# Sixteen output stores of a cross-attention and routed-FFN kernel, issued by GpSimd as indirect DMAs in place of SyncE's strided DMAs

## The chip, the cores and the metric

The kernel runs on one core of one Trainium2 chip. The metric is device time in microseconds (us) of one execution; the time given for a kernel is the median of several runs.

## The reference

What is computed, cut to its core (two batches of 1024 tokens, 256 wide, 64 context keys, 16 heads, 12 experts, the top 3 of them for each of three routers):

```
x = x + attention(layernorm(x), ctx, mask)           # Wq, Wk, Wv, Wo and their biases
xf = layernorm(x)                                    # 2048 rows of 256
C1, C2, C3 = softmax over the top 3 of (xf @ P_w.T) @ U1.T, U2.T, U3.T   # [2048, 12] each
h = gelu(sum_e C1[:, e] * (xf @ W1[e].T))
y = sum_e C2[:, e] * (h @ W2[e].T) + C3 @ b2
return x + y                                         # [2, 1024, 256] float32
```

## The kernel before

The 2048 rows are cut into T = 16 tiles of 128 rows, eight for each batch (TPB = 8). All rows lie in `x_all` [128 partitions, 16 tiles, 256]: tile t holds, on partition p, row 8p + j of batch b, with t = 8b + j. The attention stage adds its result into `x_all`, the expert stage adds the second layer's result into it, and that tile is then stored to the output.

Each engine has a program of its own, written out by hand, and the programs meet only in semaphores. After about 116 us (the attention stage) the expert stage runs, one tile in 17.75 us:

- TensorE (`experts` in the tensor block) multiplies six pairs of experts for layer 1 of tile t + 1 and six pairs for layer 2 of tile t. Each product is six matmuls of 512 columns (`split_product`, L920). Between the pairs stand small steps, among them `transpose_xf(t + 2)` (L1025), which waits for `xf`.
- VectorE (`experts` in the vector block) weighs and sums the products (`sum_pair`, L815), ends a layer with `last_sum` (L820), and between them runs the statistics of tile t + 2 (L595 to L598), `normalise2` (L602, writes `xf`), the router's `find_top` and `combine_weights` (L774 to L793, with `w_at_e` at L787) and `move_weights` (L801).
- GpSimd has three small steps for each tile, in the loop at L429: `inverse_deviation` (L355, L357, writes `rstd`, for which `normalise2` waits), `exponentials` (L406) and `split_c3` (L417, L422).
- SyncE issues all loads but three. Once the last weights are in flight, it has only the stores: `store(b, j, sums)` at L309 waits on `acc`, the count of VectorE's sums, until the tile's last sum is written, and issues one DMA of 128 rows of 1 KB (L311). Two loops run over the tiles, and the last store stands by itself. The program ends when all stores have landed (`stored` at 16 * T).

The semaphore `acc` counts SUMS = 13 per layer and tile. `later(t, n)` says that a tile number is at least n or a loop variable. `is_last(t)` picks other buffers for the last tile.

Of the kernel before, what the change touches and what calls it, by code (L numbers as in the profile page):

```python
# [14 lines left out]
P = 128  # L15
# [6 lines left out]
def xattn_ffn_kernel(nc: bass.Bass, x, mask, ctx_t, wq_t, bq, wk_t, bk, wv_t, bv, wo_t, bo,  # L22
# [56 lines left out]
    with ExitStack() as ctx:  # L79
        def sb(name, shape, dt=F32):  # L80
            return ctx.enter_context(nc.sbuf_tensor(name, shape, dt))

        def sem(name):
            return ctx.enter_context(nc.semaphore(name))
# [20 lines left out]
        head_of = sb("head_of", [P, HPC])  # L105
        head_in = sb("head_in", [P, HPG])
        iota_e = sb("iota_e", [P, EXPERTS])
        minus_half = sb("minus_half", [P, 1])
        eps = sb("eps", [P, 1])
        waited = sb("waited", [P, 1])  # L110
# [117 lines left out]
        bv_in, bo_in = sem("bv_in"), sem("bo_in")  # L228

        consts_set = sem("consts_set")  # L230
        setup_dve = sem("setup_dve")
        kt_done, v_done, g_done = sem("kt_done"), sem("v_done"), sem("g_done")
        ident_b_set, wo_hi, b2_hi = sem("ident_b_set"), sem("wo_hi"), sem("b2_hi")
# [39 lines left out]


        x_dram = x.rearrange("b (p j) d -> b p j d", j=TPB)
        out_dram = out.rearrange("b (p j) d -> p b j d", j=TPB)
        mask_dram = mask.rearrange("b (p j) k -> b p j k", j=TPB)
        rows = lambda w: w.rearrange("(c p) n -> p c n", c=C)
        w_dram = [w.rearrange("(c p) e o -> p c (e o)", c=C) for w in (w1_t, w2_t)]
# [5 lines left out]
        def _(sp):  # L285
# [20 lines left out]
                sp.dma_start(stage[:, n % RING, :, :],  # L306
                             w_dram[layer][:, :, pair * 2 * D:(pair + 1) * 2 * D]).then_inc(w_in[n % RING], 16)

            def store(b, j, sums):  # L309
                sp.wait_ge(acc, sums)  # L310
                sp.dma_start(out_dram[:, b, j, :], x_all[:, j + b * TPB, :]).then_inc(stored, 16)  # L311

            for b in range(BATCH):
                with sp.Fori(0, TPB if b < BATCH - 1 else TPB - 1) as j:
                    store(b, j, 2 * SUMS * j + (2 * SUMS * b * TPB + 3 * SUMS))
            store(BATCH - 1, TPB - 1, 2 * SUMS * T)
            sp.wait_ge(stored, 16 * T)


        @block.gpsimd  # L320
        def _(pool):
# [5 lines left out]
            pool.memset(euler[:, :], EULER).then_inc(consts_set, 1)  # L327
            pool.iota(iota_e[:, :], pattern=[[1, EXPERTS]], base=0, channel_multiplier=0,
                      allow_small_or_imprecise_dtypes=True).then_inc(consts_set, 1)
            pool.wait_ge(consts_set, 7)  # L330

            pool.affine_select(out=ident[:, :], in_=ident[:, :], compare_op=ALU.not_equal, fill=1.0, base=0,
# [70 lines left out]
            def exponentials(t):  # L403

                pool.wait_ge(route, ROUTE_STEPS * t + ROUTE_EXP)
                pool.tensor_tensor(top_e[:, :], euler[:, :], top_d[:, :, :].rearrange("p r k -> p (r k)"),  # L406
                                   ALU.pow).then_inc(e_ready, 1)

            def split_c3(t):

                if is_last(t):
                    pool.wait_ge(route, ROUTE_STEPS * T)
                else:
                    pool.wait_ge(c_moved, t + 1)
                if later(t, 1):
                    pool.wait_ge(c3t_done, t)
                pool.tensor_tensor(c3_hlh[:, 0:3:2, 0:EXPERTS].bitcast(F32R),  # L417
                                   weights2(t)[:, 2:3, :].to_broadcast([P, 2, EXPERTS]),
                                   ones[:, 0:2 * EXPERTS].rearrange("p (k e) -> p k e", k=2),
                                   ALU.mult).then_inc(c3_hi, 1)  # L420
                pool.wait_ge(c3_hi, t + 1)
                pool.tensor_tensor(c3_hlh[:, 1, 0:EXPERTS], weights2(t)[:, 2, :], c3_hlh[:, 0, 0:EXPERTS],  # L422
                                   ALU.subtract).then_inc(c3_lo, 1)

            exponentials(0)
            inverse_deviation(1, stats2_ready, var2_ready, rstd2_ready)
            exponentials(1)
            split_c3(0)
            with pool.Fori(2, T) as t:  # L429
                inverse_deviation(t, stats2_ready, var2_ready, rstd2_ready)  # L430
                exponentials(t)
                split_c3(t - 1)
            split_c3(T - 1)


        @block.scalar
# [774 lines left out]
```

## Time and profile before

| | us |
|---|---|
| median of 3 runs | 414.28 (414.12 to 414.6) |
| span of the profiled execution, first to last instruction | 412.4 |
| TensorE busy | 392.4 (95%) |
| VectorE busy | 342.9 (83%) |
| ScalarE busy | 115.8 (28%) |
| GpSimd busy | 110.9 (27%) |

The span leaves out what lies around the first and last instruction; the median of the runs is 1.88 us above it. Busy time counts neither branches, register and semaphore instructions nor the issue of DMAs. A row of the timeline reads: start in us, duration in us, engine, line, operation, output<-inputs, shape, xcount, and in brackets how long the engine was idle before and what released it. PEld is TensorE's weight load, SPq SyncE's queue.

### The profile page before, as it was taken

The page shows a single profiled execution, that of the slowest core. Times are in us where ns is not written, and L with a number is a line of the kernel's source. Part 1 is how long each engine was busy: PE and PEld are TensorE (multiplying, and loading weights), DVE is VectorE, ACT ScalarE, POOL GpSimd, SP SyncE. Part 2 cuts the span into 40 slices and gives each one's busy share as a digit, 9 for nine tenths or more (in the row PEclk, how much of TensorE's full clock was granted, in tenths as well). Part 3 has the DMA queues.
Part 4 walks back from the last instruction along what each step waited for, and adds up shares of the span by engine and source line. Part 5 has one row for each costly group of instructions (what it writes and reads, how often), then busy time and mean ns, then how long its engine had stood idle before and what let it go on. Part 6 is the DMA issues. An engine that isn't in the chain of part 4 may idle for free.

```text
span 412.4 us, 7824 instructions
## 1 busy us (share of the span) xinstructions
PE 392.4 (95%) x2132; PEld 331.0 (80%) x2132; DVE 342.9 (83%) x1036; ACT 115.8 (28%) x263; POOL 110.9 (27%) x165
## 2 busy tenths in 40 slices
PE   4499999999989999999999999999999999999996
PEld 4388988989868888888888888888888888888884
DVE  3998889889885889789897988989789898888875
ACT  3477888888822111010110101011010100101000
POOL 5462755657520220202112020211202112020200
PEclk9999999999989999999999999999999999999999
DMA  7900123131000000000000000000000000000000
GB/s 225 333 2 2 61 92 98 55 102 51 2 0 3 0 2 13 13 0 13 0 13 13 0 13 0 13 0 13 13 0 13 0 13 13 0 13 0 14 0 26
DMA packets 8612, 12.71 MB, mean 31 GB/s; under 512 B 1076, under 2 KB 5016, under 8 KB 8472
## 3 DMA queue, kind: packets, MB, share of 16 engines
q1 hardware_dynamic: 8040, 12.44, 9.1%
q10 hardware_dynamic: 560, 0.13, 0.1%
q8 instruction: 5, 0.08, 0.1%
q14 instruction: 7, 0.06, 0.0%
HBM read 10.47 MB, written 2.10 MB: 30 GB/s over the span
## 4 chain that ended last, share of the span: by engine, by line
PE 89%; DVE 4%; issue 3%; ACT 2%; DMA 1%; POOL 1%; ACTq 0%; DVEq 0%; POOLq 0%
PE banks L920 68%; PE banks L997 5%; PE banks L987 3%; PE banks L962 3%; PE banks L972 2%; PE banks L975 2%; PE banks L977 2%; PE banks L1035 1%; DMA bk_sb<-in_bk_dram 1%; PE banks L1043 1%; DVE q_hl L625 1%; PE banks L1025 1%; PE banks L1008 1%; PE banks L953 1%; DVE s_max L631 1%
## 5 line engine op out<-in xcount | busy, mean ns | idle before, releaser
L815 DVE SCALAR_TENSOR_TENSOR s_d<-banks,c_cur,s_d 128x256 f32<-128x256 f32 x165 | 72.7, 478 | 27.6 <-PE banks L920 23.1
L920 PE MATMUL banks<-w_h,xf_h 128*128 128x512 f32 x204 | 81.8, 401 | 0.0
L920 PE MATMUL banks<-w_l,xf_h 128*128 128x512 f32 x204 | 80.6, 395 | 0.0
L920 PE MATMUL banks<-w_h,xf_l 128*128 128x512 f32 x204 | 80.2, 393 | 0.0
L406 POOL TENSOR_TENSOR top_e<-euler,top_d 128x9 f32<-128x9 f32 x16 | 28.9, 1807 | 185.1 <-DVE top_d L765 185.1
L920 PE MATMUL banks<-w_h,h_h 128*128 128x512 f32 x180 | 73.5, 408 | 0.0
L920 PE MATMUL banks<-w_l,h_h 128*128 128x512 f32 x180 | 71.1, 395 | 0.0
L920 PE MATMUL banks<-w_h,h_l 128*128 128x512 f32 x180 | 71.1, 395 | 0.0
L815 DVE SCALAR_TENSOR_TENSOR sum<-banks,c_new,sum 128x256 f32<-128x256 f32 x160 | 66.6, 476 | 3.2 <-PE banks L920 3.1
L561 ACT ACTIVATE h_h<-banks 128x256 fp32r<-128x256 f32 x15 | 5.8, 385 | 156.5 <-PE banks L1043 156.5
L920 PEld LDWEIGHTS banks<-w_l,xf_h 128*128 128x128 f32 x204 | 38.6, 189 | 8.5
L920 PEld LDWEIGHTS banks<-w_h,xf_l 128*128 128x128 f32 x204 | 38.8, 190 | 7.8
L920 PEld LDWEIGHTS banks<-w_h,xf_h 128*128 128x128 f32 x204 | 38.8, 190 | 7.7
L920 PEld LDWEIGHTS banks<-w_l,h_h 128*128 128x128 f32 x180 | 33.8, 188 | 8.2
L920 PEld LDWEIGHTS banks<-w_h,h_l 128*128 128x128 f32 x180 | 33.9, 188 | 6.9
L920 PEld LDWEIGHTS banks<-w_h,h_h 128*128 128x128 f32 x180 | 33.9, 188 | 6.8
L366 POOL TENSOR_TENSOR w_l<-stage,w_h 128x1024 f32 (+1 forms) x12 | 28.8, 2397 | 32.6 <-ACT w_h L534 32.6
L997 PE MATMUL banks<-v_ext,prob_t 128*128 (+1 forms) x256 | 30.1, 273 | 0.5 <-ACT prob_t L476 0.5
L997 PEld LDWEIGHTS banks<-v_ext,prob_t 128*128 128x128 f32 x256 | 29.9, 192 | 0.7 <-issue 0.7
L571 ACT ACTIVATE xn_t<-xn 128x256 f32<-128x256 f32 x16 | 6.7, 418 | 77.3 <-DVE xn L820 77.3
L631 DVE TENSOR_REDUCE s_max<-banks 128x16 f32<-128x1024 f32 x16 | 19.6, 1223 | 5.6 <-PE banks L977 5.5
L476 ACT ACTIVATE prob_t<-banks 128x512 f32<-128x512 f32 x32 | 17.4, 594 | 17.7 <-PE banks L987 17.6
(126 smaller groups left out, 618.5 us busy)
## 6 DMA issues: line engine op xcount, KB each, us to landing
stage<-in_w_t_dram SPq DMA_DIRECT2D x12, 512.0 KB, 3.7
out_dram<-x_all SPq DMA_DIRECT2D x16, 128.0 KB, 1.9
x_all<-in_x_dram SPq DMA_DIRECT2D x1, 1024.0 KB, 8.0
x_all<-in_x_dram SPq DMA_DIRECT2D x1, 768.0 KB, 7.9
mask_all<-in_mask_dram SPq DMA_DIRECT2D x2, 256.0 KB, 5.1
x_all<-in_x_dram SPq DMA_DIRECT2D x2, 128.0 KB, 3.5
wk_sb<-in_wk_t_dram SPq DMA_DIRECT2D x1, 256.0 KB, 3.7
wq_sb<-in_wq_t_dram SPq DMA_DIRECT2D x1, 256.0 KB, 4.3
```

The source lines that it names most:

```text
L366: pool.tensor_tensor(w_l[:, n, :, :], stage[:, slot, :, :], w_h[:, n, :, :].bitcast(F32), ALU.subtract).then_inc(w_split, 1)
L406: pool.tensor_tensor(top_e[:, :], euler[:, :], top_d[:, :, :].rearrange("p r k -> p (r k)"), ALU.pow).then_inc(e_ready, 1)
L476: nc.scalar.activation(prob_t[:, j:j + HP // 2, :], ps_pt[:, j:j + HP // 2, :], ACT.Copy).then_inc(pt_copied, 1)
L631: dve.tensor_reduce(s_max[:, :], ps_s, AX_X, ALU.max).then_inc(s_maxed, 1)
L815: dve.scalar_tensor_tensor(out=sums[e % 2][:, :], in0=product, scalar=weights[:, e:e + 1], in1=sums[e % 2][:, :], op0=ALU.mult, op1=ALU.ad ...
L920: ins = pe.matmul(dst, a(c), b(c), start=(i == 0), stop=(i == len(terms) - 1))
L962: ins = pe.matmul(ps_q[:, m, :], wq_sb[:, c, m * P:(m + 1) * P], xn_t[:, c, :], start=(c == 0), stop=(c == C - 1))
L972: pe.matmul(banks[:, c, :].rearrange("p (h k) -> p h k", k=KEYS), ident_b[:, :], mask_bias[:, t, :].unsqueeze(1).to_broadcast([P, HPC, KEY ...
L975: pe.matmul(banks[:, c, group * HPG * KEYS:(group + 1) * HPG * KEYS], q_hl[:, c, group, :], kbd_hh[:, b, c, group, :, :].rearrange("p h k ...
L977: ins = pe.matmul(banks[:, c, :], q_h[:, c, :], kbd_l[:, b, c, :, :].rearrange("p h k -> p (h k)"), start=False, stop=True)
L987: ins = pe.transpose(ps_pt[:, j, :], prob[:, 2 * j:2 * j + 2, :].rearrange("p h k -> p (h k)"), ident[:, :])
L997: ins = pe.matmul(ps_v[:, j * 2 * VW:(j + 1) * 2 * VW], prob_t[:, j, :], v_ext[:, b, j, :], start=True, stop=True)
```

## The change

GpSimd fills a table `row_of` [128, 16] of row numbers once, with an iota at the start: entry (p, t) is 1024b + 8p + j. A store is now an indirect DMA that GpSimd issues: the source is tile t of `x_all`, 128 partitions of 256 floats, and each partition's row goes to the row of the output that `row_of[:, t]` names. The rows, their size and their number are those of before. SyncE's stores and its last wait are gone.

In GpSimd's program the loop over tiles 2 to 15 is written out, and iteration t ends with the store of tile t - 3. Behind it stand the last `split_c3` and the stores of tiles 13, 14 and 15, and the wait for all of them.

```
+        row_of = sb("row_of", [P, T], I32)
...
-        out_dram = out.rearrange("b (p j) d -> p b j d", j=TPB)
+        out_rows = out.rearrange("b n d -> (b n) d")
...
-            def store(b, j, sums):
-                sp.wait_ge(acc, sums)
-                sp.dma_start(out_dram[:, b, j, :], x_all[:, j + b * TPB, :]).then_inc(stored, 16)
-
-            for b in range(BATCH):
-                with sp.Fori(0, TPB if b < BATCH - 1 else TPB - 1) as j:
-                    store(b, j, 2 * SUMS * j + (2 * SUMS * b * TPB + 3 * SUMS))
-            store(BATCH - 1, TPB - 1, 2 * SUMS * T)
-            sp.wait_ge(stored, 16 * T)
...
+            pool.iota(row_of[:, :], pattern=[[SEQ, BATCH], [1, TPB]], base=0,
+                      channel_multiplier=TPB).then_inc(rows_set, 1)
+            pool.wait_ge(rows_set, 1)
             pool.wait_ge(consts_set, 7)
...
+            def store(t):
+
+                pool.wait_ge(acc, 2 * SUMS * t + 3 * SUMS if t < T - 1 else 2 * SUMS * T)
+                pool.indirect_dma_start(out=out_rows, out_offset=bass.IndirectOffsetOnAxis(row_of[:, t:t + 1], 0),
+                                        in_=x_all[:, t, :], in_offset=None).then_inc(stored, 16)
+
             exponentials(0)
             inverse_deviation(1, stats2_ready, var2_ready, rstd2_ready)
             exponentials(1)
             split_c3(0)
-            with pool.Fori(2, T) as t:
+            for t in range(2, T):
                 inverse_deviation(t, stats2_ready, var2_ready, rstd2_ready)
                 exponentials(t)
                 split_c3(t - 1)
+                if t >= 3:
+                    store(t - 3)
             split_c3(T - 1)
+            for t in range(T - 3, T):
+                store(t)
+            pool.wait_ge(stored, 16 * T)
```

Two places of GpSimd's program, each as a row before and now. The first is one iteration for a tile, in the expert stage; the names `stats2_ready`, `route`, `c_moved` and `acc` are semaphores that VectorE raises. Before, in the loop:

```order
90 L355 TENSOR_TENSOR var_eps<-mean_var,eps 128x1 [waits stats2_ready]
91 L357 TENSOR_TENSOR rstd<-var_eps,minus_half 128x1 [waits var2_ready]
92 L405 ISA
93 L406 TENSOR_TENSOR top_e<-euler,top_d 128x9 [waits route]
94 L416 REGISTER_ALU [waits c_moved]
95 L417 TENSOR_TENSOR c_hlh<-c_cur,ones 128x2x12 [waits c3t_done]
96 L422 TENSOR_TENSOR c_hlh<-c_cur,c_hlh 128x12 [waits c3_hi]
97 L429 REGISTER_ALU
98 L429 COMPARE_AND_BRANCH
```

And now, from one `split_c3` to the next iteration's `exponentials` (the line numbers are those of the changed kernel, where L413 and L418 are `split_c3`, L424 the store, L351 and L353 `inverse_deviation`):

```order
97 L413 TENSOR_TENSOR c_hlh<-c_cur,ones 128x2x12 [waits c3t_done,c_moved]
98 L418 TENSOR_TENSOR c_hlh<-c_cur,c_hlh 128x12 [waits c3_hi]
99 L424 DMA out_dram<-x_all,row_of 2048x256 [waits acc]
100 L351 TENSOR_TENSOR var_eps<-mean_var,eps 128x1 [waits stats2_ready]
101 L353 TENSOR_TENSOR rstd<-var_eps,minus_half 128x1 [waits var2_ready]
102 L402 TENSOR_TENSOR top_e<-euler,top_d 128x9 [waits route]
```

The store stands between `split_c3` and the two instructions that make the next `rstd`; the loop's register and branch instructions are gone.

The second place is the end of the program. Before, on SyncE, the last store and the end:

```order
28 L311 DMA out_dram<-x_all 128x256
29 L314 REGISTER_ALU
30 L314 COMPARE_AND_BRANCH
31 L311 DMA out_dram<-x_all 128x256 [waits acc]
32 L79 UNCONDITIONAL_BRANCH [waits stored]
```

Now, on GpSimd:

```order
170 L418 TENSOR_TENSOR c_hlh<-c_cur,c_hlh 128x12 [waits c3_hi]
171 L424 DMA out_dram<-x_all,row_of 2048x256 [waits acc]
172 L413 TENSOR_TENSOR c_hlh<-c_new,ones 128x2x12 [waits c3t_done,route]
173 L418 TENSOR_TENSOR c_hlh<-c_new,c_hlh 128x12 [waits c3_hi]
174 L424 DMA out_dram<-x_all,row_of 2048x256 [waits acc] x3
175 L79 UNCONDITIONAL_BRANCH [waits stored]
```

The last three stores and the wait for all sixteen have moved from SyncE's queue to GpSimd's, and the store of tile 12 stands ahead of the last `split_c3`.

## Rows read from the trace of the kernel before

**Rows 1.** The page: the span, and busy time of each engine.

```profile
span 412.4 us, 7824 instructions
PE 392.4 (95%) x2132; PEld 331.0 (80%) x2132; DVE 342.9 (83%) x1036; ACT 115.8 (28%) x263; POOL 110.9 (27%) x165
```

**Rows 2.** The chain that ended last, 400 to 412.4: start, us, what.

```profile
400.52 8.20 PE banks L920 x36
...
409.66 0.42 DVE x_all L820
```

**Rows 3.** TensorE's waits, 116 to 412.4: us in total, times, longest.

```profile
PE banks L920 <- DVE a_l L655: 1.6, 1, 1.6
PE banks L1035 <- DVE x_all L662: 0.6, 1, 0.6
PE banks L997 <- ACT prob_t L476: 0.5, 1, 0.5
```

**Rows 4.** The tile view of the output: stores, ns min/median/max; time to landing.

```profile
L311 SPq DMA_DIRECT2D out_dram<-x_all x16: 338/339/384, 153.8 to 410.1; - x16
...
DMA to landing us min/median/max: 1.9/1.9/2.3
```

**Rows 5.** Timeline of the end: the last store.

```profile
410.11 0.36 SPq L311 DMA_DIRECT2D out_dram<-x_all  x1
```

**Rows 6.** DMA activity, 400 to 412.4 in 40 slices of 0.31 us.

```profile
DMA  0000000006600000000010000000000000057000
```

**Rows 7.** Timeline, GpSimd, one tile of the expert stage.

```profile
313.81 0.23 POOL L417 TENSOR_TENSOR c_hlh<-c_cur,ones 128x24 fp32r<-128x24 f32 x1 [1.09 <-DVE c_cur L801]
314.12 0.21 POOL L422 TENSOR_TENSOR c_hlh<-c_cur,c_hlh 128x12 f32<-128x12 f32 x1
315.96 0.19 POOL L355 TENSOR_TENSOR var_eps<-mean_var,eps 128x1 f32<-128x1 f32 x1 [1.63 <-DVE mean_var L598]
316.23 0.55 POOL L357 TENSOR_TENSOR rstd<-var_eps,minus_half 128x1 f32<-128x1 f32 x1
```

**Rows 8.** Timeline, VectorE, the same tile.

```profile
313.00 0.43 DVE L820 TENSOR_TENSOR x_all<-s_d 128x256 f32 x1
...
313.46 0.18 DVE L801 COPY c_cur<-c_new 128x36 f32<-128x36 f32 x1
...
314.39 0.27 DVE L787 TENSOR_TENSOR w_at_e<-at_e,top_w 128x108 f32<-128x108 f32 x1
...
318.71 0.40 DVE L602 TENSOR_SCALAR xf<-x_all,mean_var,rstd 128x256 f32 x1
```

**Rows 9.** Timeline, TensorE's weight loads, the same tile.

```profile
320.39 0.26 PEld L1025 LDWEIGHTS banks<-ident,xf 128*128 128x128 f32 x2
```

**Rows 10.** Timeline, 111 to 114.5: a GpSimd and a VectorE operation side by side.

```profile
111.36 2.39 POOL L366 TENSOR_TENSOR w_l<-stage,w_h 128x1024 fp32r<-128x1024 f32 x1 [2.23 <-ACT w_h L534]
...
112.03 2.00 DVE L746 TENSOR_TENSOR xf_l<-xf_t,xf_h 128x256 fp32r<-128x256 f32 x1
```

**Rows 11.** Timeline, VectorE: the same operation with GpSimd idle.

```profile
323.29 0.41 DVE L746 TENSOR_TENSOR xf_l<-xf_t,xf_h 128x256 fp32r<-128x256 f32 x1
```

**Rows 12.** Timeline, the start: GpSimd's constants, and who needs them first.

```profile
1.33 0.14 POOL L328 IOTA iota_e<- 128x12 f32 x1
1.62 0.29 POOL L332 TENSOR_SCALAR_AFFINE_SELECT ident<-ident 128x128 f32<-128x128 f32 x1 [0.15 <-POOL iota_e L328]
...
3.59 0.31 ACT L497 ACTIVATE ident_b<-ident 128x128 bf16<-128x128 f32 x1
```

**Rows 13.** Timeline, GpSimd's last two operations.

```profile
387.58 0.24 POOL L417 TENSOR_TENSOR c_hlh<-c_new,ones 128x24 fp32r<-128x24 f32 x1 [2.24 <-PE banks L1050]
387.90 0.21 POOL L422 TENSOR_TENSOR c_hlh<-c_new,c_hlh 128x12 f32<-128x12 f32 x1
```

**Rows 14.** Timeline, TensorE's weight load for `transpose_c3` of the last tile.

```profile
395.82 0.12 PEld L1050 LDWEIGHTS banks<-ident,c_hlh 128*96 128x96 f32 x1
```

**Rows 15.** Timeline, VectorE: the last sum of tile 14.

```profile
401.35 0.42 DVE L820 TENSOR_TENSOR x_all<-s_d 128x256 f32<-128x256 f32 x1
```

More of the change, by code:

```diff
@@ L230, in xattn_ffn_kernel @@
         consts_set = sem("consts_set")
+        rows_set = sem("rows_set")
         setup_dve = sem("setup_dve")
```

## Prediction

> **What bounds the kernel now.** I read the busy times first: TensorE is at work for 392.4 of 412.4 us, and GpSimd, the engine that takes on the stores, for 110.9 [rows 1]. The waits say more than these shares. From 116 us on TensorE waits for another engine three times, 2.7 us in all, each at the passage between the stages [rows 3], so through the sixteen tiles of the expert stage the matmuls stand back to back. The chain that ended last is matmuls up to 408.72, then VectorE's sums, the last of which ends at 410.08 [rows 2]. Behind it only the last store is left: issued at 410.11, and the span ends at 412.4 [rows 1, 5]. A change to the stores can therefore cost time at two places alone: in this tail, where every part of the last store counts in full, and inside the stage, where it counts only once a delay reaches TensorE. The fifteen earlier stores of SyncE delay nobody, so taking them away gains nothing.
>
> **How far the engines can slip.** I follow one tile. GpSimd ends `split_c3` at 314.33 and has nothing until the statistics release it at 315.96: 1.63 us idle. It then makes `rstd` by 316.78, and VectorE takes that at 318.71, 1.93 us later [rows 7, 8]. VectorE ends `xf` at 319.11, and TensorE loads it at 320.39, 1.28 us later [rows 8, 9]. A store placed behind `split_c3` that holds GpSimd for X us is thus free for VectorE up to 1.63 + 1.93 = 3.56 us, and for TensorE up to 3.56 + 1.28 = 4.84 us. Each us above would be paid by TensorE in each of the twelve iterations in which another `rstd` follows a store.
>
> **The change, part by part.**
>
> *The row table at the start.* One iota more, and a wait for it. The iota of before takes 0.14 us, and the operation behind its wait starts 0.15 us after it ends; twice that at most, 0.3 us, moves `ident` from 1.91 to about 2.2 [rows 12]. The first to read `ident` is ScalarE at 3.59, so 1.4 us of slack cover it: 0. Without this cover it would be 0.3 us.
>
> *The loop written out.* It takes register and branch instructions out of a queue that waits 1.63 us in this place anyway [rows 7]: 0.
>
> *Thirteen stores inside the iterations.* The store of tile t - 3 waits on `acc`, but its tile was summed a whole iteration before `split_c3(t - 1)` is released (a tile's last sum stands just ahead of the `c_cur` copy that releases `split_c3`, at 313.00 and 313.46 in the tile shown [rows 8]; the store then takes the tile summed 17.75 us before that one), so the wait is already met and the store costs only X. Queued behind it is `inverse_deviation`, and behind that VectorE and TensorE. What is X? No row of before shows GpSimd issuing a DMA. From below: SyncE holds its queue 0.34 us for the same 128 rows [rows 4]. From above: GpSimd's longest kind of operation, on 1024 elements in each partition, takes 2.39 us in the row shown [rows 10]. The middle is 1.37, and I take 1.4, since writing out 128 row addresses by a program is neither a tiny operation nor a full pass over a large tile. Even the upper end is below 3.56, so `rstd` comes in time: 0.
>
> *Order at the end.* The store of tile 12 stands ahead of the last `split_c3`, at about 385.3. With X = 1.4 it ends near 386.7, before that `split_c3` starts at 387.58; and its result is first loaded at 395.82, 7.7 us after 388.11 [rows 13, 14]. Tile 13 goes out behind it; tile 14 is summed at 401.77 [rows 15], so its store is issued and landed well before 410. All 0.
>
> *The last store.* Before: 0.03 us from the sum to the issue, 0.36 us of issue, and the data on the DMA engines in the two slices from about 410.9 to 411.5 [rows 2, 5, 6]; the semaphore is up 1.9 us (2.3 at most) after the start of the issue [rows 4]. After: GpSimd is woken by VectorE; where it was idle and waited for `c_cur` it needed 0.17 us, from 313.64 to 313.81 [rows 7, 8], about 0.13 more than SyncE. It then needs X to describe the transfer, in place of 0.36. From then on the same 128 rows of 1 KB move and are confirmed, which I take as unchanged. The tail grows by 0.13 + (1.4 - 0.36) = 1.17 us, and by 0.1 to 2.2 us at the two ends of X. I put 0.15 on top for a path that is longer in ways the rows can't show (descriptors that are written to memory and fetched): 1.3 us.
>
> How far the issue itself differs has a price in the Trainium skill (DMA: Bandwidth & Descriptors, "Latency and other measured facts"): about 1 us to the first byte for a DMA from GpSimd against about 0.6 us from SyncE. By that the tail would grow by some 0.4 us and the time would be 414.7; no row of before can confirm it, and the figure is not said to be for 128 separate row numbers.
>
> *Sum.* Profiled execution: 412.4 + 1.3 = 413.7 us of span. With the 1.88 us by which the median of the runs lies above the span: **415.6 us**, 0.3% more.
>
> **The rivals.**
>
> *B. The issue holds VectorE (slower, much).* Rows show that a GpSimd operation can stop a VectorE operation with two inputs in SBUF: `xf_l` started at 112.03 beside a GpSimd operation that ended at 113.75, and took 2.00 us, ending 0.28 us after it, where it takes 0.41 otherwise [rows 10, 11]. The store now starts at about 314.35, and VectorE's next such operation, `w_at_e`, starts at 314.39 and ends at 314.66 [rows 8]. If the issue holds the path for all of X, `w_at_e` ends 0.11 us (108 elements, by the 0.28 for 256) after 314.35 + X, so everything behind it on VectorE is late by X - 0.2. VectorE has next to no idle time up to `xf`, so the 1.28 us of slack there is what counts. With X = 1.4 the delay is 1.2 and just fits. It decides from X = 1.48 on: each of the twelve or thirteen tiles then pays the excess. X = 1.7 gives 0.22 x 13 = 2.9 us plus a tail of 1.6: 418.8. X = 2.39 gives 0.91 x 13 = 11.8 plus 2.3: 428. Against it: the store reads only one number in each partition, and may be a moment behind `w_at_e`.
>
> The page "SBUF — State Buffer" of the Trainium skill ("Who interferes with whom") states this rule: a VectorE instruction with two SBUF inputs and a GpSimd instruction that reads SBUF exclude each other, one of them waiting until the other ends, but GpSimd instructions that only write don't count. The trace agrees with the first half (2.00 against 0.41 us); whether writing descriptors counts as reading, no run here shows.
>
> *C. GpSimd's own lateness (slower).* If X is over 4.84 us, TensorE pays 12 (X - 4.84): at 5.5 us these are 7.9 us, and with a tail of 5.4 us the time is 427.6. Nothing of before lasts so long on GpSimd (2.39 at most). A milder form is a first store that is slow once, on code that GpSimd has not run before: at two and a half times the longest row, 6 us, it costs 1.2 us once and gives 416.8 with the tail of the forecast.
>
> *D. No change that can be measured.* A measurement of this kernel can tell about 0.2%, 0.83 us, from no change. If describing the transfer takes under about 0.9 us, or is overlapped with the moving of the first rows, the tail grows by less than that: X = 0.34 gives 414.5, X = 0.8 gives 415.0. It decides below X = 0.91. For it speaks that fewer than all 128 rows need be described before the first can move; the 1.9 us of before are mostly way and confirmation, not issue [rows 4, 6].
>
> *E. Faster.* Only if the end of the program, with SyncE done early, closes sooner. Nothing in the rows points to it.
>
> *The change may not do what it says*, if the rows are cut into smaller packets. The row table gives 128 distinct rows of 1 KB for each store, as before, so I give this no chance of its own; more packets than before would show it.
>
> **How the numbers follow.** The forecast (tail alone, 415.1 to 416.8, by X from 0.91 to 2.39 and 0.2 for the landing) has 0.56. D has 0.24, B 0.12, C 0.05 and E 0.03. Slower by over 0.2% is forecast, B and C: 0.73. Within 0.2% is D: 0.24. Faster 0.03. For the range I leave out E and the fastest of D at the lower end and stop at 414.6; at the upper end I take in the forecast, C's mild form and B up to X = 1.7, and stop at 418.8. What is left out is about 0.17.
>
> **What would show it.** (1) In the stage TensorE still waits for nobody, and the final matmul ends within 0.3 us of 408.7; if B or C holds, it is later and the wait of L1025 on `xf` appears. (2) `w_at_e` keeps its 0.27 us; B would make it 1 us or more. (3) GpSimd's store has a duration near 1.4 us, and a landing near 3 us from its start, where SyncE's had 1.9. (4) The span ends 3.5 us after the last sum, in place of 2.3. (5) GpSimd's `rstd` is made at the same distance from the statistics. I am wrong if the last sum moves by more than 0.5 us, or if the tail grows by less than 0.8 or more than 2.5 us.

## The result and the profile after

| | before | after |
|---|---|---|
| median, runs on the same chip (us) | 414.44 (4 runs) | 417.17 (4 runs, 416.57 to 417.37) |
| span of the profiled execution (us) | 412.4 | 415.6 |
| from the end of the last sum to the end of the span (us) | 2.32 | 4.76 |

The change makes the kernel slower: the ratio is 1.0063, with a 95% interval of 1.0047 to 1.008. That is 2.7 us, where 1.3 was forecast. (One sentence is needed for all that follows: the executions of most kernels here fall into a main group and one that takes 1.2 to 1.7 us longer, in whose profiles TensorE's granted clock is low at 26 to 32 us; where a few tenths matter I compare main group with main group, and parts of one profile with parts of another.)

The page of after, with the answers to [rows 1]. Columns: busy time, share, instructions; for the queues packets, MB and share.

```profile
span 415.6 us, 7683 instructions
PE 395.4 (95%) x2132; PEld 333.3 (80%) x2132; DVE 341.7 (82%) x1036; ACT 115.6 (28%) x263; POOL 128.8 (31%) x182
...
q1 hardware_dynamic: 5736, 10.34, 7.8%
q0 software_dynamic: 768, 2.10, 1.4%
```

GpSimd is busy for 17.9 us more: the sixteen stores. They move 2.10 MB in 768 packets, 48 for each store. SyncE's queue q1 has 2304 packets fewer than before (8040 there), which were 144 for each store; the rows were not cut smaller.

TensorE's waits from 116 us on, as [rows 3]: the same three, of the same length.

```profile
PE banks L927 <- DVE a_l L662: 1.6, 1, 1.6
PE banks L1042 <- DVE x_all L669: 0.6, 1, 0.6
PE banks L1004 <- ACT prob_t L483: 0.5, 1, 0.5
```

One tile of the expert stage on GpSimd, as [rows 7], now with the store between `split_c3` and `rstd`:

```profile
314.43 0.23 POOL L413 TENSOR_TENSOR c_hlh<-c_cur,ones 128x24 fp32r<-128x24 f32 x1 [1.00 <-DVE c_cur L808]
314.74 0.21 POOL L418 TENSOR_TENSOR c_hlh<-c_cur,c_hlh 128x12 f32<-128x12 f32 x1
315.12 1.15 POOL L424 DMA_INDIRECT out_dram<-x_all,row_of  x1 [0.17 <-issue]
316.64 0.18 POOL L351 TENSOR_TENSOR var_eps<-mean_var,eps 128x1 f32<-128x1 f32 x1 [0.38 <-DVE mean_var L605]
```

The store holds GpSimd from 315.12 to 316.27, and GpSimd is then idle for 0.38 us again, waiting for the statistics. The 1.63 us of [rows 7] had room for it, and `rstd` is not late at all.

The tile view of the output, as [rows 4]: the time that GpSimd is held, in ns (min, median, max), and the time from the start of the issue to the landing.

```profile
L424 POOL DMA_INDIRECT out_dram<-x_all,row_of x16: 960/1150/1299, 173.0 to 411.1; - x16
...
DMA to landing us min/median/max: 2.6/2.8/3.0
```

The end of the chain that ended last, as [rows 2]:

```profile
410.42 0.44 DVE x_all L827
410.85 0.27 issue
411.12 0.96 POOL out_dram L424
```

And the instructions that close each queue, those of line L79, on GpSimd after the change (duration in ns, start in us):

```profile
L79 POOLq COMPARE_BRANCH  x1: 41/41/41, 413.8 to 413.8; - x1
L79 POOLq DRAIN  x1: 1382/1382/1382, 413.9 to 413.9; - x1
```

The same view of before, where SyncE was the last:

```profile
L79 SPq COMPARE_BRANCH  x1: 38/38/38, 412.0 to 412.0; - x1
L79 SPq DRAIN  x1: 7/7/7, 412.2 to 412.2; - x1
L79 POOLq DRAIN  x1: 326/326/326, 387.9 to 387.9; - x1
```

**Where the 3.2 us of span went.** The tail grew by 2.44 us, in three pieces. From the last sum to the issue: 0.28 us in place of 0.03, so +0.25. From the start of the issue until the engine is released by the landing: 411.12 to 413.8, 2.7 us, in place of 410.11 to 412.0, 1.9 us, so +0.8. From there to the end of the span: 1.8 us in place of 0.4, so +1.4. The last is nearly all one instruction. Each queue ends with a DRAIN; SyncE's takes 0.007 us, GpSimd's 1.38 us, and since GpSimd is now the engine that waits for the last landing, its DRAIN lies behind everything. (The 326 ns of GpSimd's DRAIN in the kernel before begin at 387.9, while its last operation runs until 388.11 [rows 13].)

The remaining 0.76 us is the later end of the last sum, 410.84 for 410.08. Little of it came from the expert stage: from the first `top_e` to the last sum it takes 292.5 us before (from 117.56) and 292.7 after (from 118.14). The other 0.58 us were there at 118 us already. Part of that may be the execution that was profiled: TensorE's granted clock at 17 to 20 us was 0.62 in it, and 1.00 in that of before.

### The profile page after: what moved, and what is told of

Same layout as the page of the kernel before. It is cut to its first block, busy times and chain, and to the rows that moved or that the text cites. A ratio compares the mean times of both kernels' runs of the same rounds, so it can differ in the third digit from the quotient of the medians.

```text
span 415.6 us, 7683 instructions
## 1 busy us (share of the span) xinstructions
PE 395.4 (95%) x2132; PEld 333.3 (80%) x2132; DVE 341.7 (82%) x1036; ACT 115.6 (28%) x263; POOL 128.8 (31%) x182
## 4 chain that ended last, share of the span: by engine, by line
PE 89%; DVE 4%; ACT 2%; issue 2%; POOL 1%; DMA 1%; ACTq 0%; DVEq 0%; POOLq 0%
PE banks L927 67%; PE banks L1004 5%; PE banks L969 3%; PE banks L994 3%; PE banks L979 2%; PE banks L982 2%; PE banks L984 2%; PE banks L1042 1%; DMA bk_sb<-in_bk_dram 1%; PE banks L1050 1%; DVE q_hl L632 1%; PE banks L1032 1%; PE banks L1015 1%; PE banks L960 1%; DVE s_max L638 1%
## 5 line engine op out<-in xcount | busy, mean ns | idle before, releaser
L402 POOL TENSOR_TENSOR top_e<-euler,top_d 128x9 f32<-128x9 f32 x16 | 28.9, 1808 | 185.5 <-DVE top_d L772 185.5
L424 POOL DMA_INDIRECT out_dram<-x_all,row_of x16 | 18.0, 1127 | 22.4 <-DVE x_all L827 19.8
```

The costliest lines, as they stand in the source:

```text
L424: pool.indirect_dma_start(out=out_rows, out_offset=bass.IndirectOffsetOnAxis(row_of[:, t:t + 1], 0), in_=x_all[:, t, :], in_offset=None).t ...
```

## The experiments

Theory A (that of the prediction): the cost is the issue of a DMA by GpSimd, 128 row addresses written out by a program, plus a little of landing. Theory B, formed on the profile after: about half of it is the DRAIN of GpSimd, which is work that depends on what GpSimd has issued. (These letters are not those of the prediction's rivals, nor those in the expectation of e4.) The start is a third, small question. All kernels compute the full output. Each ratio is against runs of the kernel before made beside it.

| run | what stores | median us (range, runs) | ratio, 95% | tail us | GpSimd's DRAIN us |
|---|---|---|---|---|---|
| before | SyncE | 414.13 to 414.22, in three rounds | | 2.32 | 0.33, hidden |
| e1 | 15 GpSimd, last SyncE | 415.33 (414.34 to 416.26, 10) | 1.0019, 1.0 to 1.0037 | 2.47 | 1.301, hidden |
| e2 | 16 GpSimd, plain | 416.6 (416.32 to 417.78, 10) | 1.0053, 1.0036 to 1.007 | 4.35 | 1.375 |
| e3 | 15 SyncE, last GpSimd | 416.12 (415.87 to 417.5, 10) | 1.0048, 1.0028 to 1.0067 | 3.79 | 0.149 |
| e4 | 16 GpSimd, SyncE waits | 417.4 (415.86 to 417.72, 10) | 1.0064, 1.0043 to 1.0084 | 3.89 | beside the landing |
| e5 | 16 GpSimd, earlier in the tile | 418.37 (416.91 to 418.46, 4) | 1.009, 1.007 to 1.0111 | 4.78 | 1.382 |
| e6 | 13 stores in 4 pieces | 424.55 (424.31 to 424.83, 4) | 1.0242, 1.022 to 1.0265 | 7.9 | 4.567 |
| e7 | 13 stores in 8 pieces | 513.0 (512.03 to 514.54, 4) | 1.2366, 1.2338 to 1.2394 | 12.1 | 8.814 |
| e8 | SyncE, row table kept | 415.93 (414.23 to 416.4, 12) | 1.0023, 1.0007 to 1.0038 | 2.43 | 0.324, hidden |
| e9 | e1, GpSimd waits too | 416.18 (415.92 to 417.41, 4) | 1.0057, 1.0037 to 1.0077 | 3.8 | 1.301 |
| e10 | the changed kernel again | 417.02 (416.79 to 418.62, 6) | 1.0063, 1.0044 to 1.0082 | 4.69 | 1.382 |
| e11 | half each | 417.34 (416.44 to 418.23, 4) | 1.007, 1.0048 to 1.0091 | 4.03 | 0.729 |
| e12 | 16 GpSimd, drained before the last | 416.45 (415.57 to 417.28, 4) | 1.0062, 1.0042 to 1.0082 | 3.47 | 0.129 |

The tail is the time from the end of the last sum to the end of the span in the profiled execution. It is the sharper measure: the medians also carry the start.

### Only the last store goes back to SyncE

```
+            sp.wait_ge(acc, 2 * SUMS * T)
+            sp.dma_start(out_dram[:, BATCH - 1, TPB - 1, :], x_all[:, T - 1, :]).then_inc(stored_sp, 16)
+            sp.wait_ge(stored_sp, 16)
...
-            for t in range(T - 3, T):
+            for t in range(T - 3, T - 1):
                 store(t)
-            pool.wait_ge(stored, 16 * T)
+            pool.wait_ge(stored, 16 * (T - 1))
```

> The changed kernel, with the store of the last tile given back to SyncE as a strided DMA; GpSimd waits for its own fifteen stores only. Theory (the tail): the whole cost is behind the last sum, namely 0.25 us of waking, 0.8 us of longer landing and a drain of GpSimd's queue of 1.38 us after the last landing. Then this kernel has SyncE's tail again, 2.3 us from the last sum to the end, GpSimd's drain ends long before, and the time is that of the kernel before, within 0.3 us. Rival (the stage): the thirteen stores inside the iterations cost part of it, through GpSimd, VectorE or the DMA engines; then 0.3 to 1 us over the kernel before stay. Second rival (a fixed cost of having software DMAs at all): 1.4 us or more stay.

The tail is 2.47 us (411.83 to 414.3), that of before within 0.15, although fifteen stores are still indirect ones of GpSimd. Its DRAIN, in the view of the instructions of L79, has not gone; it only has cover:

```profile
L79 POOLq DRAIN  x1: 1301/1301/1301, 406.6 to 406.6; - x1
```

So the fifteen stores inside the stage are free, and the tail's cost belongs to the last store and to what GpSimd does behind it. e1 is the nearest to before; in the main group of its executions it is about 0.4 us over it, which is the question of e8.

### All sixteen by GpSimd, but as plain strided DMAs

```
-                pool.indirect_dma_start(out=out_rows, out_offset=bass.IndirectOffsetOnAxis(row_of[:, t:t + 1], 0),
-                                        in_=x_all[:, t, :], in_offset=None).then_inc(stored, 16)
+                pool.dma_start(out_dram[:, t // TPB, t % TPB, :], x_all[:, t, :]).then_inc(stored, 16)
```

> The changed kernel with the sixteen stores still issued by GpSimd, but as plain strided DMAs, without row numbers (the row table is still filled). Theory: the cost belongs to the software path of GpSimd, not to the row numbers. Tail again about 4.8 us, the same drain of about 1.4 us, and the time within 0.4 us of the changed kernel; the issue may be shorter than 1.15 us (0.8 to 1.1). Rival: the row numbers are what costs (reading them, one description per row); then the issue falls to 0.4 us or less and the time falls by 1 us or more.

The tile view of the output:

```profile
L424 POOL DMA_DIRECT2D out_dram<-x_all x16: 542/628/789, 172.3 to 410.5; - x16
...
DMA to landing us min/median/max: 2.2/2.3/2.5
```

The issue takes little more than half as long, 0.63 us, less than the 0.8 to 1.1 that I had expected, and the tail is 4.35 us in place of 4.76. The row numbers thus cost 0.4 us; the other 2.0 us over the tail of before are there without them, a DRAIN of 1.375 us among them.

### Only the last store by GpSimd, as an indirect one

```
 # against the kernel before; the row table is filled as in the change
-                sp.dma_start(out_dram[:, b, j, :], x_all[:, j + b * TPB, :]).then_inc(stored, 16)
+                sp.dma_start(out_dram[:, b, j, :], x_all[:, j + b * TPB, :]).then_inc(stored_sp, 16)
...
-            store(BATCH - 1, TPB - 1, 2 * SUMS * T)
-            sp.wait_ge(stored, 16 * T)
+            sp.wait_ge(stored_sp, 16 * (T - 1))
...
+            store(T - 1)
+            pool.wait_ge(stored, 16)
```

> The kernel before, with only the last tile's store given to GpSimd as an indirect DMA; the other fifteen stay with SyncE, and GpSimd's loop is a loop again. Theory (the tail): all of the cost is back, 2.4 us over the kernel before by the tail's parts. The issue is a first one here, so it may take 1.3 us in place of 0.96. Rival (the stage): less than 2 us. Rival (the drain works off all sixteen stores): the drain is much shorter than 1.38 us, and the time 1 to 1.5 us over the kernel before.

The instructions of L79 on GpSimd:

```profile
L79 POOLq DRAIN  x1: 149/149/149, 413.9 to 413.9; - x1
```

By theory A the whole cost should be here, because the last store is, and I had expected 2.4 us over before. It isn't: the tail is 3.79 us, 1.47 over before and 0.97 less than after, although this one issue took 1.235 us, 0.27 more than the last one of after (0.96). The DRAIN takes 0.149 us in place of 1.382, 1.23 less; with the 0.27 more of issue this makes the 0.97. So the DRAIN's length comes from the DMAs that GpSimd issued before.

### SyncE waits for the sixteen landings

```
             # SyncE
+            sp.wait_ge(stored, 16 * T)
             # GpSimd
-            pool.wait_ge(stored, 16 * T)
```

> The changed kernel, but SyncE waits for the sixteen landings in place of GpSimd; GpSimd goes into its drain right after the last issue. Theory A (the drain is GpSimd's own work after an issue): it runs beside the landing and is over before it, so the span ends about 0.4 us after the landing, and 1.3 us of the 2.4 are gone. Theory B (the drain waits for the DMA's completion and then takes 1.38 us): nothing is gained, within 0.2 us.

The closing instructions of GpSimd and of SyncE:

```profile
L79 POOLq DRAIN  x1: 3579/3579/3579, 410.3 to 410.3; - x1
L79 SPq DRAIN  x1: 7/7/7, 413.3 to 413.3; - x1
```

GpSimd now enters its DRAIN without waiting for the landing; its 3.58 us even begin ahead of the store's own row (410.5), so they hold the issue too. The tail is 3.89 us: 0.87 of the 1.38 us are won, and GpSimd still ends 0.5 us after SyncE. If all of the DRAIN's work could lie beside the landing, the tail would be 3.4. The issue ends at 411.45; 1.38 us of work from there would be over at 412.8, and the DRAIN ends at 413.9, 0.8 us behind the landing. So neither reading of the expectation came out: more was gained than nothing and less than 1.3 us. How much of the work has to come behind the landing, this run doesn't tell.

### Is it the number of DMAs, or how recent they are?

e9 is e1, with GpSimd made to wait for SyncE's last store as well, so that GpSimd's last DMA was issued 10 us before the DRAIN begins, in place of 3.

```
             # on top of e1
             pool.wait_ge(stored, 16 * (T - 1))
+            pool.wait_ge(stored_sp, 16)
```

> As with the last store given back to SyncE, but GpSimd too waits for that store's landing before it goes to the end, so its drain starts when the last software DMA is 7 us old. Theory (the drain is work that depends on how many DMAs GpSimd has issued since the start: 1.38 us after sixteen, 1.30 after fifteen, 0.15 after one): the drain takes 1.3 us again and lies on the path; the tail from the last sum to the end is 2.3 + 1.3 = 3.6 to 3.8 us. Rival (the drain is slow only behind a DMA that has just landed): it takes under 0.3 us and the tail is 2.4 to 2.6 us.

The instructions of L79 on GpSimd, e9:

```profile
L79 POOLq DRAIN  x1: 1301/1301/1301, 412.9 to 412.9; - x1
```

It takes the same 1301 ns as at 406.6, and the tail goes from 2.47 to 3.8: the 1.3 us have lost their cover. The last store, its issue and its landing are those of before. Age doesn't matter, and one more wait in a program cost 1.3 us.

e11 halves the number: even tiles by SyncE, odd ones (with the last) by GpSimd.

```
+            for t in range(0, T, 2):
+                sp.wait_ge(acc, 2 * SUMS * t + 3 * SUMS)
+                sp.dma_start(out_dram[:, t // TPB, t % TPB, :], x_all[:, t, :]).then_inc(stored_sp, 16)
...
-                if t >= 3:
+                if t >= 3 and (t - 3) % 2:
...
-            for t in range(T - 3, T):
+            for t in (T - 3, T - 1):
...
```

> Stores in turn: the eight even tiles by SyncE as strided DMAs, the eight odd tiles, the last among them, by GpSimd as indirect DMAs. Theory (about 0.085 us of drain for each DMA that GpSimd has issued, from 0.15 at one to 1.38 at sixteen): a drain of 0.15 + 7 x 0.082 = 0.72 us, a tail of 4.1 us, 0.65 us less than with sixteen. Rival (a step: any DMA beyond the first brings the full price): 1.38 us and a tail of 4.7.

The same view of e11:

```profile
L79 POOLq DRAIN  x1: 729/729/729, 415.1 to 415.1; - x1
```

With 1, 8, 15 and 16 DMAs the DRAIN takes 0.149, 0.729, 1.301 and 1.38 us. The steps are (0.729 - 0.149) / 7 = 0.083 and (1.301 - 0.729) / 7 = 0.082 us for each DMA. The tail, 4.03 us, is 0.73 less than after's. Each of these DMAs describes 128 rows, so the runs don't tell a price for each DMA from a price for each row described.

### The same work, drained earlier

```
             for t in range(T - 3, T):
+                if t == T - 1:
+                    pool.wait_ge(stored, 16 * (T - 1))
+                    pool.drain()
                 store(t)
```

> The changed kernel with one drain of GpSimd's queue put ahead of the last store, behind a wait for the fifteen earlier landings, where GpSimd is idle for 7 us. Theory (the drain works off what has been issued since the last drain): that early drain takes 1.3 us under cover, the one at the end 0.15 us, the tail falls from 4.76 to 3.5 us and the time by 1.2 us. Rival (the price is that of the last drain as such, or of the number of DMAs in the whole program): the last drain keeps 1.38 us and nothing is gained.

A drain fits in, since GpSimd is idle for 7.35 us ahead of its last store. Timeline of GpSimd, after:

```profile
411.12 0.96 POOL L424 DMA_INDIRECT out_dram<-x_all,row_of  x1 [7.35 <-DVE x_all L827]
```

The added drain (L441) and the closing one (L79) on GpSimd, e12:

```profile
L441 POOLq DRAIN  x1: 1300/1300/1300, 405.0 to 405.0; - x1
...
L79 POOLq DRAIN  x1: 129/129/129, 413.4 to 413.4; - x1
```

The added drain takes the 1.3 us, from 405.0 to 406.3, long before the last sum. The final DRAIN has 0.129 us left, and the tail is 3.47 us, 1.29 less than after's, from one wait and one drain more. This is theory B's strongest test: nothing is taken away, the work is only done where nobody waits for it. In the main group of executions e12 takes 415.57 to 415.8 (two executions), the changed kernel 416.8 to 417.1; the ratios over all executions, 1.0062 and 1.0063, don't show the gain, since two of e12's four fell in the longer group. What is left against before, 3.47 - 2.32 = 1.15 us, is the wake-up, the issue and the longer way of the last store. It is the best of the kernels in which GpSimd makes all sixteen stores; none of the versions beats the kernel before.

### Does the issue hold VectorE?

In after, `w_at_e` had started before the store (315.05 to 315.32, the store from 315.12), so the rival of the prediction, in which the store starts first, was not put to the test by the change itself. e5 puts the store ahead of `split_c3`, where VectorE has operations with two inputs in SBUF.

```
-                split_c3(t - 1)
                 if t >= 3:
                     store(t - 3)
+                split_c3(t - 1)
```

> The changed kernel with the thirteen stores of the iterations put ahead of split_c3 in place of behind it, so that they start when the exponentials are done and run beside VectorE's operations with two SBUF inputs (at_e, top_w, w_at_e; 0.27, 0.17 and 0.27 us in the changed kernel). In the changed kernel the store starts only after w_at_e has, so it tells nothing of the rival that the issue holds VectorE. If it does: one of the three lasts 0.5 us or more, VectorE is late by 0.5 to 1.1 us in each tile, under the 1.28 us of slack, so the time stays. If it does not: all three keep their durations to 0.03 us. In both cases split_c3 is 0.3 to 1.2 us later, with slack, and the time is that of the changed kernel within 0.3 us.

Timeline, GpSimd and VectorE, one tile of the expert stage:

```profile
314.68 1.07 POOL L424 DMA_INDIRECT out_dram<-x_all,row_of  x1 [0.18 <-issue]
...
314.78 0.42 DVE L827 TENSOR_TENSOR x_all<-s_d 128x256 f32 x1
...
315.34 0.27 DVE L781 TENSOR_TENSOR at_e<-top_i,iota_e 128x108 f32<-128x108 uint32 x1
```

Both VectorE operations run wholly beside the store (314.68 to 315.75), and at their usual pace: 0.42 us for the sum, which took 0.43 in [rows 8], and 0.27 for `at_e`, as long as `w_at_e` in [rows 8], of the same 108 elements. The rival B is refuted. `w_at_e` takes 0.31 us in e5, 0.04 longer than elsewhere; it runs from 316.13, behind the store and beside the second operation of `split_c3`. The Trainium skill ("SBUF — State Buffer", "Who interferes with whom") says that GpSimd instructions which only write don't exclude such an operation; the issue of a store behaves like one of them, although it reads a row number in each partition. Three of the four timed executions of e5 were of the longer group; the lowest, 416.91, is that of the changed kernel.

### How long may GpSimd be held?

The prediction allowed 4.84 us before TensorE pays [rows 7 to 9]. e6 and e7 cut the thirteen stores inside the stage into 4 and 8 indirect DMAs of 64 and 32 columns.

```
+                n = D // pieces
+                for c in range(pieces):
+                    pool.indirect_dma_start(out=out_rows,
+                                            out_offset=bass.IndirectOffsetOnAxis(row_of[:, t:t + 1], 0),
+                                            in_=x_all[:, t, c * n:(c + 1) * n], in_offset=None,
+                                            element_offset=c * n).then_inc(stored, 16)
...
-                    store(t - 3)
+                    store(t - 3, 4)                  # e7: 8
...
```

> The changed kernel, each of the thirteen stores inside the iterations cut into four indirect DMAs of 64 columns, so that GpSimd is held about four times as long: 4 x 1.15 + 3 x 0.2 = 5.2 us. The slack by the rows of before is 4.84 us from the end of split_c3, and the store starts 0.4 us behind it. Theory (slack and queue as predicted): TensorE waits for xf in twelve iterations, 5.2 + 0.4 - 4.84 = 0.75 us each, 9 us in all; the drain after 55 DMAs grows by 39 x 0.082 = 3.2 us; together 12 us over the changed kernel, 429. Rival 1 (VectorE absorbs the delay): no wait at TensorE, only the 3.2 us of drain. Rival 2 (a piece of 256 B rows is issued much faster than one of 1 KB rows): hold under 4 us, no wait.

e6, timeline of GpSimd in one tile:

```profile
299.46 1.13 POOL L426 DMA_INDIRECT out_dram<-x_all,row_of  x1 [0.17 <-issue]
300.90 0.97 POOL L426 DMA_INDIRECT out_dram<-x_all,row_of  x1 [0.30 <-issue]
...
303.44 0.96 POOL L426 DMA_INDIRECT out_dram<-x_all,row_of  x1 [0.30 <-issue]
304.42 0.20 POOL L351 TENSOR_TENSOR var_eps<-mean_var,eps 128x1 f32<-128x1 f32 x1
```

Behind the first, the indirect DMAs follow each other every 1.27 us. From the end of `split_c3` at 299.29 until `rstd` can be begun, GpSimd is held for 0.17 + 4.94 us, 0.27 over the 4.84. TensorE's wait for `xf` appears in the timeline of its weight loads:

```profile
305.84 0.20 PEld L1036 LDWEIGHTS banks<-ident,xf 128*128 128x128 f32 x2 [0.46 <-DVE xf L613]
```

The stage grows by about 4.5 us, 0.38 for each of twelve iterations. I had expected 9, from a hold of 5.2 us; with the hold that was measured the bound, 0.27 us, comes out within about 0.1 us for each tile. The instructions of L79 on GpSimd, e6:

```profile
L79 POOLq DRAIN  x1: 4567/4567/4567, 417.8 to 417.8; - x1
```

55 DMAs: 0.149 + 54 x 0.082 = 4.58 us by the steps of e3 and e11, 4.567 measured. The packets don't set it: these 55 DMAs make 1808, 2.4 times after's 768, and the DRAIN is 3.3 times after's.

> The same with eight pieces of 32 columns: GpSimd is held 8 x 1.15 + 7 x 0.2 = 10.6 us in each of the thirteen iterations. Theory: TensorE loses 10.6 + 0.4 - 4.84 = 6.2 us in each of twelve, 74 us in all; the drain after 107 DMAs takes 0.15 + 106 x 0.082 = 8.9 us, 7.5 more than in the changed kernel; together about 82 us over it. If the price line holds at four pieces and at eight, the 4.84 us of slack were read rightly. Rival: the drain does not grow with the count beyond sixteen (1.4 to 2 us).

TensorE's waits from 116 us on, of e7:

```profile
PE banks L1036 <- DVE xf L613: 47.1, 9, 5.4
PE banks L1036 <- issue: 15.6, 3, 5.2
```

They sum to 62.7 us, where 12 x (0.17 + 9.99 - 4.84) = 64 follows from the bound. The DRAIN takes 8.814 us; 107 DMAs give 0.149 + 106 x 0.082 = 8.84. But the median is 98.8 us above before, and waits and tail make only some 73 of it. The windows of TensorE around one gap (us, busy time and matmuls, granted clock, DMA share, GB/s) show the rest:

```profile
305.00:310.00 5.00, 1.12 (x6) 1.00 0.06 13
310.00:315.00 5.00, 3.69 (x10) 0.52 0.01 3
315.00:320.00 5.00, 5.00 (x21) 0.80 0.00 0
320.00:325.00 5.00, 5.00 (x23) 1.00 0.01 2
```

And the timeline of its matmuls behind that gap:

```profile
311.31 0.69 PE L1036 MATMUL banks<-ident,xf 128*128 128x128 f32 x2 [5.20 <-DVE xf L613]
...
312.23 0.63 PE L931 MATMUL banks<-w_h,h_l 128*128 128x512 f32 x1
312.65 0.63 PE L931 MATMUL banks<-w_l,h_h 128*128 128x512 f32 x1
...
317.21 0.39 PE L931 MATMUL banks<-w_h,h_l 128*128 128x512 f32 x1
```

After 5.2 us without work TensorE comes back at the lower of its two clocks, with a matmul every 0.43 us instead of 0.23, until about 316.9. The thirteen matmuls of that stretch come 0.2 us later each than they would, 2.6 us in this tile in addition to the gap; over the twelve tiles the remaining 26 us are 2.2 for each. In e6, where the matmuls wait for `xf` 0.3 us at the longest, the granted clock is 1.00 in every window from 160 us on.

### The start: the row table alone

```
 # against the kernel before
+            pool.iota(row_of[:, :], pattern=[[SEQ, BATCH], [1, TPB]], base=0,
+                      channel_multiplier=TPB).then_inc(rows_set, 1)
+            pool.wait_ge(rows_set, 1)
```

> The kernel before, with only the row table filled at the start and waited for; all stores by SyncE, the table unused. Theory: ident is 0.2 to 0.3 us later under 1.4 us of slack, nothing follows, the time is that of the kernel before in the same group of granted clock, within 0.2 us. Rival (the start): the share of executions with a low early clock goes up from about a quarter to about a half, and the median moves by 0.3 to 1.3 us with it.

Timeline of before, the first matmul and the first `top_e` of the expert stage:

```profile
5.25 1.19 PE L928 MATMUL banks<-ctx_sb,wk_sb 128*128 128x128 f32 x4 [5.25 <-DMA bk_sb<-in_bk_dram]
...
117.56 1.81 POOL L406 TENSOR_TENSOR top_e<-euler,top_d 128x9 f32<-128x9 f32 x1 [3.82 <-DVE top_d L765]
```

The same of e8:

```profile
5.36 1.19 PE L933 MATMUL banks<-ctx_sb,wk_sb 128*128 128x128 f32 x4 [5.36 <-DMA bk_sb<-in_bk_dram]
...
118.04 1.81 POOL L411 TENSOR_TENSOR top_e<-euler,top_d 128x9 f32<-128x9 f32 x1 [3.82 <-DVE top_d L770]
```

And of e12, which has the same table at its start:

```profile
5.05 1.19 PE L938 MATMUL banks<-ctx_sb,wk_sb 128*128 128x128 f32 x4 [5.05 <-DMA bk_sb<-in_bk_dram]
...
117.61 1.81 POOL L402 TENSOR_TENSOR top_e<-euler,top_d 128x9 f32<-128x9 f32 x1 [3.81 <-DVE top_d L775]
```

Nothing but the table differs from before, and the tail is before's (2.43 us). Yet `top_e` begins 0.48 us later in e8, and in the main group its executions take 414.23 to 414.75, those of before 413.87 to 414.42: medians 0.5 us apart, not within the 0.2 that I had expected. The traces of the other kernels with the table temper this. In e2, e4, e6 and e12 the first `top_e` begins at 117.56 to 117.62, where before has it. Part of the scatter is the first loads, whose landing releases the first matmul at 4.98 to 5.36 us. Counted from that matmul, `top_e` comes after 112.31 us in before, and after 112.50 to 112.73 in the seven profiles of the main group with the table (e2, e3, e4, e6, e8, e9, e12), 112.84 in that of after. So 0.2 to 0.4 us go with the table and not with the stores; but before has only one profile, so that the table causes them is likely and not shown, and by what way is open. The path that the prediction followed is not it: ScalarE reads `ident` at 3.60 us in e8, at 3.59 before.

The granted clock early on doesn't explain it either. At 15 to 17 us it is 1.00 in before and 0.50 in e8, but 0.50 also in e4, whose `top_e` begins at 117.56. What marks the profiles of the longer group (e1, e5, e7, e10, e11, with `top_e` at 118.95 to 119.40) is a second stretch, at 26 to 32 us, where all others have 1.00. TensorE's window of e1 (columns as for e7):

```profile
26.00:29.00 3.00, 2.35 (x8) 0.64 0.00 0
```

Of e8's twelve executions seven fell in the longer group, of before's seventeen six. Over all runs it is 16 of 59 for before and about 32 of 78 for the kernels with the table (e6 and e7 left out). That is a tendency, and no proof that the table brings it about.

### The changed kernel again

No edit.

> The changed kernel once more, on the same chip and beside the same runs of the kernel before as the next three. Theory (the tail): 2.4 us over the kernel before when executions with the same granted clock are compared (main group of both, clock 0.990 or more). Rival (the start): in addition, the changed kernel falls more often than the kernel before into executions in which TensorE's clock is granted low early on (clock 0.983 to 0.987, 1.5 us longer), which moves its median by up to 1 us more.

417.02 us, ratio 1.0063: the first result over again, beside seventeen runs of before. In the main group it is 416.79 to 417.12 against 413.87 to 414.42, 2.84 us: 2.44 of tail, and 0.4 that lie ahead of the last sum.

## Why the prediction was right in sign and short in size

The time fell into the range (414.6 to 418.8), and "slower", with 0.73, came true. The likeliest value, 415.6, was 1.6 us short. That the range held is in part luck: 417.17 lies above the 415.1 to 416.8 of the forecast itself, in the part that was kept for rival B, and B did not happen; what cost the time there was a term that the prediction did not have. By its steps:

- **Two places only, tail and stage.** The tail was rightly named. The list may have missed a third place, the start, with 0.2 to 0.4 us (e8).
- **4.84 us of slack.** Right. e6 and e7 put it to the test: a hold of 5.11 us delays a tile by 0.38, one of 10.16 by 5.2. It is the best-founded number of the prediction, and it came from a few rows of one tile.
- **The row table: 0.** Probably 0.2 to 0.4 us too low, by the traces with the table; not settled. The cover of 1.4 us ahead of `ident_b` held, but it was argued from one consumer: the step followed only the first reader of `ident` and not what else GpSimd does at the start.
- **The loop written out: 0.** Nothing contradicts it; no run isolates it.
- **X = 1.4 us for the issue.** 1.15 in the stage and 0.96 for the last: 0.25 to 0.44 too high, inside its bounds, and free inside the stage as said.
- **Thirteen stores in the stage: 0.** Right within 0.2 us: 292.7 us against 292.5, and TensorE waits as before.
- **Wake-up 0.13.** It was 0.25.
- **Issue +1.04 and 0.15 on top, landing unchanged.** Together 1.19 forecast, 0.8 measured. Two errors in part cancel: the engine is held for only 0.96 us, and the way behind it takes 1.7 us where it took 1.5.
- **Behind the landing: nothing.** This is the step that failed. The sum ended with the last landing, as if every engine closed its program alike. [rows 1, 5] can't show the closing instructions, but the trace of before does: a DRAIN of 7 ns on SyncE and one of 326 ns on GpSimd, and no DMA of GpSimd before it. So it could show that the two engines close differently, and not the price. The DRAIN adds 1.4 of the 2.44 us, more than any term that I had.

In short: forecast 0.13 + 1.04 + 0.15 = 1.3 us; measured 0.25 + 0.8 + 1.4 of tail, and 0.4 ahead of it, 2.85.

Of the signs that were named: (1) the last matmul stayed late by 0.76 us and not within 0.3, but no wait on `xf` appeared, so it was not a rival's sign: 0.58 of it was there at 118 us; (2) held, and e5 shows it where the overlap is real; (3) was met with 1.15 and 2.8 us; (4) the span ends 4.76 us after the last sum, not 3.5; (5) held. Of the two conditions for being wrong, the last sum moved by 0.76 us in the profile of after, over the 0.5 that I allowed, so by that condition I was wrong (in e2, e4 and e12 it moved by 0.13 to 0.25), and the tail grew by 2.44, just under the 2.5.

Rival B is refuted by e5; C is right as a bound (e6, e7) and didn't arise, and its mild form neither: the first store took 1.30 us, where the median is 1.15, not 6. D fell, though X was close to its threshold of 0.91: with the tail's 0.25 + 0.8 alone it would have been nearly right. E had the end of the program in view, with the wrong sign. The price in the Trainium skill (DMA: Bandwidth & Descriptors, "Latency and other measured facts"), 0.4 us more to the first byte, is matched by the plain DMAs of e2, which land 2.3 us after the start of their issue, against 1.9 [rows 4]; the indirect ones need 2.8.

## What to carry to other kernels

Follow the path of an edit to the last instruction of the program, past the last landing: when a wait moves to another engine, what that engine does at its end moves with it. If GpSimd has issued DMAs and is the last to finish, let another engine make the last store, or drain GpSimd once where it is idle; inside a stage, its DMAs are free as long as they fit the idle time in front of what is queued behind them. A slack worked out from a few rows of a timeline (idle time, plus the distance to each next consumer) predicts well from which hold on an engine delays TensorE.

## What the runs showed of the hardware

- GpSimd's DRAIN grows with the number of DMAs it has issued since the last one: 0.149 us after 1, 0.729 after 8, 1.301 after 15, 1.38 after 16 (indirect or plain), 4.567 after 55 and 8.814 after 107, in a straight line of 0.082 us each. Their age (e9) and bytes (e6, e7) make no difference. All had 128 rows, so a price for each row is not told apart from one for each DMA. A drain in between takes the debt away: 0.129 us were left in e12.
- An indirect DMA of 128 rows holds GpSimd for 0.96 to 1.30 us, a plain one of the same rows for 0.54 to 0.79 (SyncE 0.34, [rows 4]). Back to back the indirect ones come every 1.27 us, with rows of 256 as with rows of 128 bytes.
- The issue doesn't slow VectorE's operations with two inputs in SBUF (e5).
- After a gap of 5.2 us TensorE came back at the lower of its two clocks, until about 316.9 in the tile shown (e7); where it waited 0.3 us at the longest, the granted clock was 1.00 (e6).
